# A block's residual moved from VectorE to ScalarE and an accumulating DMA, with token loads issued earlier

## What is computed

```python
mod = (_silu(L0_c) @ L0_wmod).reshape(B, 6, 1, -1)       # sa, ca, ga, sb, cb, gb
ga = (2 * (ga >= 0) - 1) * jnp.maximum(jnp.abs(ga), 0.25) # gb likewise
h = _layernorm(x) * (1 + ca) + sa
# attention part: Q = relu(rope(h @ W_Q)); H = tanh(Q + hh_b)
#   out = group_norm_rows(H) * gn_weight + gn_bias    (32 groups of 16 channels)
#   out = swapaxes(out, -2, -1).reshape(B, T, C)      (a transposition read back as rows)
x = x + ga * out
h = _layernorm(x) * (1 + cb) + sb
# FFN part: gate, up, down weights are lut[idx], idx of 1376 x 512, lut of 16 values
x = x + gb * (down @ (silu(gate @ h) * (up @ h)))
```

## Time and profile before

| | us |
|---|---|
| median of three runs | 1008.93 |
| profiled execution | 1010.04 |
| its span | 1008.2 |
| TensorE busy | 924.3 (92%) |
| VectorE busy | 597.6 (59%) |
| ScalarE busy | 432.1 (43%) |
| GpSimd busy | 137.1 (14%) |

### The profile page before, as it was taken

The page is one execution under the profiler, slowest core; times in us unless marked ns, Lnnn a source line. Parts: engine busy times, 40 slices in busy tenths (PEclk is TensorE's granted clock), DMA queues, the critical chain, the costliest instruction groups (busy, mean ns, idle before and its releaser), DMA issues.

```text
span 1008.2 us, 12879 instructions
## 1 busy us (share of the span) xinstructions
PE 924.3 (92%) x4364; PEld 431.8 (43%) x4364; DVE 597.6 (59%) x1379; ACT 432.1 (43%) x652; POOL 137.1 (14%) x127
## 2 busy tenths in 40 slices
PE   4948668868999999999999999999999999999998
PEld 1324334333444444444444444444444444444443
DVE  5988989994899983338988863322223332222312
ACT  2475757468877742256255233312223331222200
POOL 3011202033333321122022001100000110000000
PEclk9969788989999999999999999999999999999999
DMA  8658365720000032240533314230000212000001
GB/s 283 189 125 230 99 193 167 236 78 32 22 21 26 15 136 84 92 136 13 167 72 98 81 47 194 74 104 0 0 0 1 73 42 95 0 0 0 11 32 42
DMA packets 33738, 83.44 MB, mean 83 GB/s; under 512 B 2848, under 2 KB 2976, under 8 KB 30624
## 3 DMA queue, kind: packets, MB, share of 16 engines
q1 hardware_dynamic: 32544, 74.54, 22.4%
q0 software_dynamic: 1152, 8.39, 4.5%
HBM read 64.04 MB, written 18.87 MB: 82 GB/s over the span
## 4 chain that ended last, share of the span: by engine, by line
PE 68%; DVE 16%; ACT 6%; issue 5%; DMA 5%; SPq 0%; POOL 0%; DVEq 0%; ACTq 0%
PE ps L1211 33%; PE ps L1247 22%; PE ps L1200 4%; DMA xa<-x_dram 4%; PE ps L1178 3%; DVE hid L846 3%; DVE st L765 2%; PE ps L1166 2%; PE ps L1223 2%; DVE R L832 1%; ACT xa L493 1%; ACT w_all L555 1%; ACT h L503 1%; PE ps L1258 1%; DMA w_all<-wmod_dram 1%
## 5 line engine op out<-in xcount | busy, mean ns | idle before, releaser
L1211 PE MATMUL ps<-h,w_all 128*128 128x512 f16 x1920 | 416.5, 379 | 3.3 <-ACT w_all L555 2.5
L1211 PEld LDWEIGHTS ps<-h,w_all 128*128 (+1 forms) x1920 | 187.7, 98 | 229.5 <-ACT w_all L555 3.0
L1247 PE MATMUL ps<-w_all,hid 128*128 128x512 f16 x1056 | 229.7, 379 | 0.4 <-DVE w_all L1093 0.4
L1247 PEld LDWEIGHTS ps<-w_all,hid 128*128 128x128 f16 x1056 | 103.3, 98 | 123.9 <-issue 0.9
L889 DVE SCALAR_TENSOR_TENSOR hd<-ps,col,sg 128x512 f32<-128x512 f32 x80 | 59.9, 749 | 128.7 <-ACT sg L525 128.3
L525 ACT ACTIVATE sg<-ps,col 128x512 f32<-128x512 f32 x80 | 54.8, 685 | 170.6 <-PE ps L1211 170.3
L914 DVE SCALAR_TENSOR_TENSOR hd<-ps,col,gbB 128x512 f32<-128x512 f32 x32 | 24.0, 751 | 140.5 <-PE ps L1247 140.1
L493 ACT ACTIVATE xa<-xa,ln_sb 128x512 f32<-128x512 f32 x60 | 44.0, 805 | 125.9 <-DVE ln_sb L775 125.9
L1200 PE MATMUL ps<-hid,w_all 128*128 128x512 f16 x352 | 89.1, 415 | 8.1 <-DVE hid L846 8.0
L540 ACT ACTIVATE hid<-hd 128x512 f16<-128x512 f32 (+1 forms) x88 | 55.0, 628 | 85.7 <-DVE hd L889 69.7
L1178 PE MATMUL ps<-WQ,work 128*128 128x512 f16 x384 | 85.4, 379 | 6.3 <-DVE work L794 3.2
(11 more groups left out here) (116 smaller groups left out, 766.1 us busy)
## 6 DMA issues: line engine op xcount, KB each, us to landing
R<-x_dram SPq DMA_DIRECT2D x16, 1024.0 KB, 6.9
xa<-x_dram SPq DMA_DIRECT2D x14, 1024.0 KB, 5.6
hid<-idx_dram SPq DMA_DIRECT2D x44, 256.0 KB, 5.5
R<-bias_dram POOLq DMA_DIRECT2D x8, 1024.0 KB, 9.0
out_dram<-R SPq DMA_DIRECT2D x32, 256.0 KB, 2.2
x_dram<-R SPq DMA_DIRECT2D x7, 1024.0 KB, 5.1
w_all<-wmod_dram SPq DMA_DIRECT2D x6, 1024.0 KB, 13.2
h<-idx_dram SPq DMA_DIRECT2D x11, 256.0 KB, 2.6
```

What stands on the lines that cost most here:

```text
L1211: ins = nc.tensor.matmul(bank(GU[2 * s + t]), W[wp][:, bass.ds(at, P)], h2[hp][:, s, k], start=(k == 0 and i == 0), stop=(k == K - 1 and i ...
L1247: ins = nc.tensor.matmul(bank(QY[par]), hid[hp][:, bass.ds(at, P)], W[wp][:, w_at:w_at + BLK], start=(j == 0 and i == 0), stop=(j == J - 1 ...
```

## The change

All of it lies in the attention of batch 0. The residual of blocks 0, 1 and 2 leaves VectorE. In its place ScalarE copies each transposed part out of PSUM with the scale `gnw` into `bias_rows[0]` (free once the bias has been stored, or once the previous adding has landed), and GpSimd adds these rows to `R` with an accumulating DMA (`add_g_rows`), which waits for the adding of the bias. Block 3 keeps VectorE's residual. SP's store waits for the new semaphore `g_added`. The token load moves ahead of that wait, by one block. On GpSimd, `split_lo(q)` now stands ahead of the bias adding, and the bias of block 0 and of block 1 are added behind `split_lo(1)`. In block 0, VectorE does `rope_relu(3)` and `stats(1)` ahead of `center(1)`, and ScalarE does `norm(1)` ahead of `square(1)` and `make_bias(0)`.

```diff
@@ sync
-                if 0 < q < NB - 1:
-                    load_x(x_toks[0, q + 1], q + 1)
                 if q + 1 < NB:
                     reach(sp, x2_out, 16 * q)
                     load_rows((q + 1) % 2, rows_of_block(0, q + 1))
...
                     load_idx(w, w % 2)
+                if q + 2 < NB:
+                    load_x(x_toks[0, q + 2], q + 2)
                 for s in ((), (SB,), (CB, GB), ())[q]:
                     load_mod(s)
                 if not last:
-                    sp.wait_ge(x2_ready, K * (q + 1))
+                    sp.wait_ge(g_added, 16 * (q + 1))
@@ gpsimd
-            for q in range(NB - 1):
+            def add_g_rows(q):
+
+                pool.wait_ge(x2_ready, K * (q + 1))
+                pool.wait_ge(rows_added[q % 2], 16 * (q // 2 + 1))
+                nc.gpsimd.dma_start(R[q % 2][:], bias_rows[0], accum_op=ALU.add).then_inc(g_added, 16)
+
+            for q in range(1, NB):
+                split_lo(q, hq[0], hq[1])
+                if q == 1:
+                    add_bias_rows(0, 0)
                 add_bias_rows(q, 0)
-                split_lo(q + 1, hq[0], hq[1])
-            add_bias_rows(NB - 1, 0)
+                add_g_rows(q - 1)
@@ scalar
+            def weighted_g(q):
+
+                if q:
+                    act.wait_ge(g_added, 16 * q)
+                else:
+                    act.wait_ge(bias_out, 16)
+                for k in range(K):
+                    act.wait_ge(gt_ready, K * q + k + 1)
+                    nc.scalar.activation(bias_rows[0][:, k * C:(k + 1) * C], bank(TB[k % 2]), ACT.Copy,
+                                         scale=gnw[:, k:k + 1]).then_inc(x2_ready, 1)
...
                 summed_out(w + 2, 0)
                 if not last:
                     summed_out(w + 3, 1)
+                    weighted_g(q)
                     half_idx(w + 6, 0)
@@ vector
-                    center(q, 1)
                     rope_relu(q, q, 3)
+                    stats(q + 1)
+                    center(q, 1)
...
-                residual(q, half, (xa[:, A - 1], xb[:, A - 1]) if last else ())
+                    residual(q, half, (xa[:, A - 1], xb[:, A - 1]))
```

More of the change, by code:

```diff
@@ L207, in build @@
         mod_mm = sem("mod_mm"); mod_copied = sem("mod_copied"); gate_made = sem("gate_made")
+        g_added = sem("g_added")
         silu_c = sem("silu_c"); vec_mm = sem("vec_mm"); row_mm = sem("row_mm")
@@ L604, in attn_block @@
                     half_idx(w + 3, 1)
-                square(q, 1)
-                if q == 0:
                     tanh(q, 3)
+                    norm(q + 1)
+                    square(q, 1)
+                    summed_out(w, 0)
                     act.wait_ge(row_ready, 1)
                     make_bias(0)
-                if not last:
-                    norm(q + 1)
-                if q:
+                else:
+                    square(q, 1)
+                    if not last:
+                        norm(q + 1)
                     tanh(q, 3)
-                summed_out(w, 0)
+                    summed_out(w, 0)
                 square(q, 2); square(q, 3)
@@ L1035, in attn_block @@
                     masks(w + 1, 1)
+                    rope_relu(q, q, 3)
+                    stats(q + 1)
                     center(q, 1)
-                    rope_relu(q, q, 3)
                 else:
@@ L1040, in attn_block @@
                     rope_relu(q, q, 0); rope_relu(q, q, 1); center(q, 0); rope_relu(q, q, 2); center(q, 1)
-                if not last:
+                if q and not last:
                     stats(q + 1)
```

## The result

The changed kernel takes 1019.84 us (median of four runs, 1018.46 to 1020.83) against 1009.17 us in the same runs of the kernel before: ratio 1.0103, 95% interval 1.0086 to 1.0121. That is +10.7 us where +6.5 was forecast; the direction was right, the size short by 4.2. In the experiments further down, one execution of e1 that took 1965.65 us, beside nine of 1005.35 to 1007.98, is left out of the ratio.

A forecast was written before the change was run, and what follows sets the result against it. Bound up to 249.7 us by a chain of waits hopping between VectorE, ScalarE, TensorE and transfers. Block 0, boundaries and loads +3.4, index chunk +3.1: +6.5 us, hence 1015.4 us; range 1009.5 to 1020.5.

The forecast's parts named there:

- The signs named beforehand: Included weighted_g 2.4 us behind the sums, TensorE idle 2.3 us, no stats wait, half_idx of block 1 waiting 1 to 6.
- T: Moment of VectorE's first rope_relu instruction of a block; forecast 7.3 us behind the end of the sums.
- GpSimd's gap: GpSimd's 10.87 us pause ahead of split_lo(1) in block 0: should go but give nothing, bounds 0 to −1.
- Residual: Boundaries between blocks: copies stand behind ScalarE's drains; loss 0.7 us into block 1, 1.3 each into blocks 2 and 3.
- Block 0: ScalarE's new order in block 0: work lands behind norm(1), path 1.8 us later, bounds 0.9 to 3.1.
- Early loads: Token loads issued earlier: the wait disappears; gain 0.6 and 1.8 us, loss 0.7 in block 3.
- Index chunk: Chunk 8, behind SP's wait for G's adding, lands at 110.6 against 107.5 wanted by ScalarE: 3.1 us late.
- Rival 2: Faster: copies run during the sums, hiding the residual's path and freeing VectorE; −3.5 us, 1005.4; chance 0.13.
- Rival 1: Only the residual's longer path costs, indices arrive in time; +3.4 us, 1012.3; chance 0.22.
- Rival 3: Late index repeats: chunk 8 by 8 us, 12 by 4, 16 by 1 to 2; central 1020; chance 0.17 with rival 4.
- chunks 12 and 16: Later index chunks behind the same SP wait: 12 just on time, 0 to 1 us late; 16 hidden.
- rival 4: Token load still late because an index chunk ahead of it on SP waits; +9 us, 1018; chance counted with Rival 3.

The follow-up runs named there:

- e1: Kernel before with only the token load moved: issued for block q+2 behind the index loads, ahead of the residual's wait; 1006.65 us, ratio 0.9969.
- e3: Changed kernel with the four weighted copies ahead of the last summed_out of a block instead of behind it; 1013.97 us, ratio 1.0045 to the kernel before.
- e10: Kernel before with only a tiny GpSimd addition behind partition_all_reduce; 1006.9 us, ratio 0.9973.
- e4: Changed kernel with make_bias(0) back ahead of norm(1) and both first bias addings ahead of split_lo(1); 1018.08 us, ratio 1.0086 to the kernel before.
- e12: e8 with GpSimd adding G of the block before ahead of the next bias adding; 1007.37 us, ratio 0.9966 to the kernel before.
- e9: Kernel before with the early token load, tiny GpSimd addition, and block 0's order as changed but make_bias(0) ahead of norm(1); 1005.20 us, ratio 0.9956.
- e2: Changed kernel with the residual of all blocks back on VectorE and no adding of G; 1018.28 us, ratio 1.0082 to the kernel before.
- e7: Changed kernel without the accumulating transfer of G, ScalarE's weighted copies kept; 1018.05 us, ratio 1.0075 to the kernel before.
- e11: e7 with the weighted copies ahead of the last summed_out; 1007.42 us, ratio 0.9981 to the kernel before.
- e6: Changed kernel with token loads of blocks 2 and 3 in 8 KB pieces instead of 2 KB (other tokens); 1018.21 us, ratio 1.0093 to the kernel before.
- e8: Changed kernel with weighted copies ahead of the last summed_out, make_bias(0) and first two bias addings early, and a tiny GpSimd addition behind partition_all_reduce; 1006.61 us, ratio 0.9973.

## Why the prediction was right, and where it fell short

The direction and the range were right, and the residual's path was right in cause and size. That the size came out near is in part luck: in block 1 two terms were wrong, and their errors met. The wait for the index chunk, +3.1, was not there, and the wait for the tokens, put at −0.6, was +3.9. The first stage came out 8.0 us longer, where 6.5 were forecast; 2.0 us more had no term at all.

**The signs named beforehand.** Seen: `weighted_g` 2.5 us behind the sums, TensorE idle for 2.33 us, T 7.1 to 7.3 behind the sums, SyncE waiting for G's adding, GpSimd's gap gone. Not seen: `stats` without a wait for a transfer (it waited 4.42) and `half_idx` of block 1 with one (it waited 0.90 us for VectorE). The FFN's first matmul was 8.0 us later with no index waited for, which lies between the signs of rivals 1 and 3.

**Residual, right.** The forecast had `project` 4.5 us behind the sums and rope 7.3; measured 4.4 and 7.1 to 7.3, at +1.1 and +1.2 us for the boundaries into blocks 2 and 3 (1.3 forecast). e3 shows the cause, the place behind `summed_out`.

**Block 0, right in size.** +2.8 against +2.5 at the rope of block 1. `norm(1)` came 0.9 us sooner (1.3 forecast). `affine(1)` began 1.9 us later (67.85 instead of 65.95), as forecast (1.8). The parts were not tested one by one.

**GpSimd's gap, wrong.** "It gives nothing" was read from `project(1)` waiting for the sums and not for `split_lo(1)`. e10 shows 2.7 us in the kernel before. By its rows the gap reached the path through the masks built meanwhile, through the time at which the next transfer left, and through the clock; these three were not tested apart. What its going is worth in the changed kernel is not shown: there the time from `affine(1)` to the end of the sums did not shrink (11.65 us, before 11.15).

**Early loads, half wrong; this is the term that failed.** Block 3's load gave 1.6 us (1.8 forecast) and e1 shows that the early load alone is worth 3.3 us. But "the wait disappears" failed for block 2: the term was −0.6 and came out at +3.9. I had counted that the addings land later in a crowd, and not how much later the load would land because of them. With one exception its landing went by how many addings ran beside it:

| addings beside the load (of block 2, where not said otherwise) | us to landing |
|---|---|
| none, but G's issued 0.3 and 1.0 us before the landing (e4; e12, load of block 3) | 7.5, 5.8 |
| one (e1, e9) | 12.7, 13.6 |
| two (e2, e7) | 17.5, 18.1 |
| two (e11) | 8.1 |
| three (changed, e3) | 22.6, 23.7 |
| three, load in 8 KB pieces (e6) | 10.3 |

An adding that is issued later costs less: with G 5.5 us behind it the load of block 2 took 7.7 and 7.5 us (e8, e12), and with a bias beside it and G 4.6, 4.7, 6.4 and 8.0 us behind it the load of block 3 took 16.4, 15.4, 14.3 and 12.5 (e8, e3, e4, changed kernel).

From e4's 7.5 on, the table has about 5 us for each megabyte added, which is what one adding holds the 16 engines for (68.4% of 22.7 us, divided by three, is 5.2 us). e11 is the exception: the same two addings, and 8.1 us. So the dose says how late the load can be made, and not that it will be; with each kernel profiled once, how often it escapes is unknown. The rows for this were there: the earlier trace rows gave the addings' landings, and the load's own rose from 5.6 (median) to 10.74 beside one of them and the store.

**Index chunk, right but hidden.** Forecast landing 110.6 (0.4 of it by a slip, since 97.0 and 5 are 102.0 and not 102.4); the store at 99.33 and the index loads at 103.92 with 6.3 us to land give 110 to 111 in the changed kernel. It is 5.15 us late as soon as the load is not (e6); 3.1 was forecast. In the changed kernel `stats` was late itself, so ScalarE did not wait. The two terms should have been taken as a maximum, both counted from the rope of block 1, and not as a sum. With the load's true landing in the place of both, the forecast would have been 3.4 + 0.6 + 3.9 = 7.9 us.

**Clock, missing.** The last 2.0 us were priced nowhere. 1.7 of them are the stretch at 1.2 GHz behind the FFN's first matmul. Only one execution of the changed kernel was profiled, so how often the clock falls there is open. In e4, e6 and e7 the falls inside `project` took back a good part of what the mended transfer gave: the three `project`s together lasted 3.4, 4.2 and 4.9 us longer than in the changed kernel.

**The rivals.** Rival 2 (faster) was excluded at its own point: the first copy ended 3.2 us behind the sums, not 0.7; e3 moved it forward: `project` began 2.4 and 2.5 us behind the sums of blocks 0 and 1, and the rope of block 2 came 0.7 us sooner behind the sums than before, where the rival said 0.6. Rival 1's mechanism is e7, in which no transfer is waited for; its +3.4 became +7.6; e11 against e7 puts down most of the difference to the clock, which fell three times. Rival 3 did not happen: chunks 12 and 16 were in time. In rival 4, `load_x` was issued in time; it was late for another reason.

The shortest landing of any adding in these runs was 7.2 us (e4), the longest 18.0 (e6). By the fit in the Trainium skill, "DMA: Bandwidth & Descriptors", section on the anatomy of one DMA on the SWDGE path (2.0 us plus bytes/436e3), it would be an estimated 4.4 us; it held for none of them.

## What to carry to other kernels

A transfer moved earlier is only early if what runs beside it at its new time is counted: here a load in short pieces paid up to the whole engine time of every long-piece transfer beside it (22.6 us for three), and in the one execution profiled the same load in long pieces did not (10.3). It was not so each time: once, with two beside it, the load in short pieces was through after 8.1 us. When a residual or any drain moves to another engine, look at what already stands in front of it in that engine's order; here 2.4 us of drains in front of four copies made `project` 1.8 us later, although 2.9 us of work had left VectorE. And two late transfers in the same block hide each other, so mending the one that the trace names may return nothing.

## What the runs showed of the hardware that was not expected

- GpSimd paused once ahead of its first ordinary instruction behind `partition_all_reduce`, with nothing to wait for in the profile: 10.87 us before and 11.63 us in e4, where that is `split_lo(1)`, and 7.55 us in e10, where it is the tiny addition. Behind the tiny addition the pause ahead of `split_lo(1)` was gone. Moving it was worth 2.7 us in the kernel before.
- An idle time of 2.33 us on TensorE was followed by a fall of the clock in some executions and not in others of nearly the same kernel; 0.4 to 1.3 us never was. Some four microseconds of change in the time of such a kernel can be that alone (e7 against e11: 9.5 us in ratio for an edit whose own path is 1.9 us at each of three boundaries).
